# A vision tower on one core: products with Wo in another bank, and three changes of order in attention

## The reference, cut to what matters

```python
h = tokens(x)                                   # 8 x 256 x 512, a state space model's kernel
h = concat([class token, h], axis=1)            # 8 x 257 x 512
h = h + attention(layernorm(h))                 # 16 heads of 32, then out @ Wo.T + bo
h = h + mixture(layernorm(h))                   # 8 experts, the two best of each token

def attention(x):
    q, k, v = x @ Wq.T + bq, x @ Wk.T + bk, x @ Wv.T + bv
    q, k = q * cos(rot), k * sin(rot)
    attn = softmax(q @ k.T / sqrt(32) * spiral)   # by head
    return (attn @ v) @ Wo.T + bo
```

## Time and profile before

| | |
|---|---|
| median of 3 runs | 771.75 us (770.42 to 772.37) |
| the profiled execution | 771.67 us, its span 769.9 us |
| PE busy | 677.3 us, 88% of the span |
| PE weight loads | 544.7 us, 71% |
| DVE busy | 531.5 us, 69% |
| ACT busy | 406.9 us, 53% |
| POOL busy | 148.0 us, 19% |
| mean granted clock of PE | 0.958 |

### The profile page before, as it was taken

The page is one execution under the profiler, slowest core; times in us unless marked ns, Lnnn a source line. Parts: engine busy times, 40 slices in busy tenths (PEclk is TensorE's granted clock), DMA queues, the critical chain, the costliest instruction groups (busy, mean ns, idle before and its releaser), DMA issues.

```text
span 769.9 us, 16642 instructions
## 1 busy us (share of the span) xinstructions
PE 677.3 (88%) x5653; PEld 544.7 (71%) x5654; DVE 531.5 (69%) x1217; ACT 406.9 (53%) x1060; POOL 148.0 (19%) x305
## 2 busy tenths in 40 slices
PE   3758887879999999999999999888479999998898
PEld 3447777867768687777867778655368888886686
DVE  4989795376778678687777777678784444446575
ACT  3835554476767667576766667666513333333111
POOL 5000000110111121111111020021122222227460
PEclk9889999999999999999999999999659999999899
DMA  7400336400001000000100002306716755557794
GB/s 226 160 0 1 139 88 147 112 1 2 3 14 42 0 27 28 27 27 14 41 0 27 27 14 96 111 29 218 274 55 199 207 165 164 164 163 229 240 324 149
DMA packets 54552, 76.11 MB, mean 99 GB/s; under 512 B 24665, under 2 KB 26969, under 8 KB 54386
## 3 DMA queue, kind: packets, MB, share of 16 engines
q1 hardware_dynamic: 41394, 42.56, 17.0%
q0 software_dynamic: 5920, 19.40, 9.8%
q10 hardware_dynamic: 7200, 13.63, 4.7%
HBM read 45.42 MB, written 30.16 MB: 98 GB/s over the span
## 4 chain that ended last, share of the span: by engine, by line
PE 69%; DVE 19%; issue 4%; ACT 3%; DMA 3%; POOL 1%; SPq 0%; DVEq 0%; ACTq 0%; POOLq 0%
PE ps L1939 43%; PE ps L2042 7%; PE ps L2052 4%; PE ps L2035 4%; PE ps L2092 4%; DVE ring L1376 3%; DVE ring L1377 3%; PE ps L1886 2%; DVE negmax L1447 2%; PE ps L2059 1%; DMA b_in<-in_L_tok_B_ri_dram 1%; PE ps L1930 1%; ACT prb L1006 1%; PE ps L2311 1%; DVE ew_lo L1686 1%
## 5 line engine op out<-in xcount | busy, mean ns | idle before, releaser
L1014 ACT ACTIVATE pts<-ps 128x512 f32<-128x512 f32 x128 | 77.2, 603 | 106.4 <-PE ps L2042 106.4
L1006 ACT ACTIVATE prb<-ps,negmax 128x257 f32<-128x257 f32 x256 | 117.9, 479 | 5.1 <-DVE negmax L1447 4.2
L1447 DVE TENSOR_REDUCE negmax<-ps 128x2 f32<-128x514 f32 x128 | 82.5, 686 | 30.7 <-PE ps L2035 30.7
L2042 PE MATMUL ps<-ident,prb 128*128 128x128 f32 x512 | 83.3, 286 | 6.2 <-DVE prb L1456 2.0
L2042 PEld LDWEIGHTS ps<-ident,prb 128*128 128x128 f32 x512 | 56.9, 143 | 30.6 <-issue 11.9
L1456 DVE TENSOR_SCALAR prb<-prb,rrec 128x258 f32<-128x258 f32 x256 | 73.5, 351 | 2.3
L1177 ACT ACTIVATE rows<-ps 128x512 f32<-128x512 f32 x40 | 23.9, 598 | 84.5 <-DVE ps L1798 84.5
L1939 PE MATMUL ps<-ew_hi,xnT_hi 128*128 x160 | 66.8, 418 | 0.1
L1939 PE MATMUL ps<-ew_lo,xnT_hi 128*128 x160 | 63.5, 397 | 0.0
L1939 PE MATMUL ps<-ew_hi,xnT_lo 128*128 x160 | 63.3, 396 | 0.0
L1886 PE MATMUL ps<-ident,ring 128*128 128x128 f32 x384 | 47.7, 281 | 15.7 <-DVE ring L1377 14.1
(11 more groups left out here) (391 smaller groups left out, 1760.9 us busy)
## 6 DMA issues: line engine op xcount, KB each, us to landing
y_slots<-rows ACTq DMA_DIRECT2D x40, 256.0 KB
ew<-in_L_ffn_expert_w_dram SPq DMA_DIRECT2D x8, 1024.0 KB, 8.5
h_dram<-h_ob SPq DMA_DIRECT2D x17, 256.0 KB, 2.0
xn_dram<-tok SPq DMA_DIRECT2D x17, 256.0 KB, 2.2
h_late<-h_dram SPq DMA_DIRECT2D x15, 256.0 KB
out_dram<-h_late SPq DMA_DIRECT2D x14, 256.0 KB
y_slots<-u_sb SPq DMA_DIRECT2D x9, 256.0 KB, 6.9
tok_dram<-so SPq DMA_DIRECT2D x4, 512.0 KB, 3.5
```

What stands on the lines that cost most here:

```text
L1006: e = act.activation(prb[:, u % 2, j, 0:KEYS], ps[:, j, 0:KEYS], ACT.Exp, bias=negmax[:, u % 2, j:j + 1], accum_out=rowsum[:, u % 2, j:j + 1])
L1014: act.activation(pts[:, slot:slot + 2, :, st * P:(st + 1) * P], ps[:, 4, :].rearrange("p (h t s) -> p h t s", h=2, t=HALVES), ACT.Copy).th ...
L1447: dve.tensor_reduce(negmax[:, u % 2, 2 * b:2 * b + 2], ps[:, 2 * b:2 * b + 2, 0:KEYS], AX_X, ALU.max, negate=True).then_inc(s["dve_max"], 1)
L2042: mm = pe.transpose(ps[:, 4, (2 * j + tt) * P:(2 * j + tt + 1) * P], prb[:, u % 2, 2 * b + j, tt * P:(tt + 1) * P], ident[:, :])
```

## The change

- `project` for the first token half of batches 0 to 6 becomes `project_first_half`, into bank 5: the twelve products with Wo first, the class value's product last. It waits for the low parts of `oT` at its start and for `pclsT` before its last product, and no longer for `ptc`. `residual` of that half reads bank 5. `pv(c, 0)` of unit 5, which writes bank 5, waits for this residual.
- `project` for the second half waits for `ptc` and no longer for the first half's residual. `project` in general waits for the low parts only before its last three products.
- In unit 3 the token tile is turned ahead of `key_turn` and `cls_turn`.
- In the last batch DVE takes the low parts (`lo_ot`) ahead of `keep_xnT(6)` in unit 6 and ahead of `take_logits(0)` in unit 7.

```diff
@@ def before_norm(c, u, first, last):
-                if last and u in (4, 5, 6):
+                if last and u in (4, 5):
                     keep_xnT(2 * u - 6)
-                if last and u == 7:
-                    dve.wait_ge(s["loaded_router"], 32)
-                    dve.wait_ge(s["pool_routing_const"], 18)
-                    take_logits(0)
...
                 if u == 4 and not first:
-                    residual(c - 1, 0, 6)
+                    residual(c - 1, 0, 5)
...
                 if u == 6:
                     lo_ot(c, 0)
-                    if not last:
+                    if last:
+                        keep_xnT(6)
+                    else:
                         lo_qk(c + 1, 1)
                 if u == 7:
...
                     lo_ot(c, 1)
-                    if not last:
+                    if last:
+                        dve.wait_ge(s["loaded_router"], 32)
+                        dve.wait_ge(s["pool_routing_const"], 18)
+                        take_logits(0)
+                    else:
                         lo_qk(c + 1, 3)
@@ def project(c, st, bank):
                 pe.matmul(ps[:, bank, :], pclsT[:, w], u_rows[:, :], start=True, stop=False)
                 for ic in range(KC):
+                    if ic == KC - 1:
+                        pe.wait_ge(s["dve_oT_low"], (c + 1) * KC)
                     mm = split3(ps[:, bank, :], (oT_hi[:, ic, w], oT_lo[:, ic, w]),
                                 (woT_hi[:, ic, :], woT_lo[:, ic, :]), False, ic == KC - 1)
                 mm.then_inc(s["pe_projected"], 1)
+
+            def project_first_half(c, bank):
+                pe.wait_ge(s["dve_oT_low"], (c + 1) * KC)
+                for ic in range(KC):
+                    split3(ps[:, bank, :], (oT_hi[:, ic, 0:P], oT_lo[:, ic, 0:P]),
+                           (woT_hi[:, ic, :], woT_lo[:, ic, :]), ic == 0, False)
+                pe.wait_ge(s["dve_key_probs"], 2 * (c + 1))
+                pe.matmul(ps[:, bank, :], pclsT[:, 0:P], u_rows[:, :], start=False, stop=True
+                          ).then_inc(s["pe_projected"], 1)
@@ tensor: def body(c, first, last):
                     if u == 3:
-                        pe.wait_ge(s["dve_cls_step"], 3 * c + 3)
-                        if not first:
-                            key_turn(c - 1)
-                        cls_turn(c)
                         if last:
                             turn_xn(0)
                         else:
                             pe.wait_ge(s["act_v_kept"], c * HALVES + 2)
                             pe.wait_ge(s["dve_xhat"], (c + 1) * HALVES + 1)
                             x_turn(7, 0)
+                        pe.wait_ge(s["dve_cls_step"], 3 * c + 3)
+                        if not first:
+                            key_turn(c - 1)
+                        cls_turn(c)
...
                         if first:
                             pe.wait_ge(s["dve_spread"], 3 + 2 * KC)
+                        else:
+                            pe.wait_ge(s["dve_residual"], c * HALVES - 1)
                         pv(c, 0)
...
                     if u == 3 and not first:
-                        pe.wait_ge(s["dve_key_probs"], 2 * c)
-                        pe.wait_ge(s["dve_oT_low"], c * KC)
+                        project_first_half(c - 1, 5)
+                    if u == 4 and not first:
                         pe.wait_ge(s["dve_cls_pT"], c + 1)
-                        project(c - 1, 0, 6)
-                    if u == 4 and not first:
-                        pe.wait_ge(s["dve_residual"], c * HALVES - 1)
                         project(c - 1, 1, 6)
@@ after the last batch:
             pe.wait_ge(s["dve_key_probs"], 2 * NB)
-            pe.wait_ge(s["dve_oT_low"], NB * KC)
             project(last, 0, 6)
             project(last, 1, 7)
```

## The result

| | before | after |
|---|---|---|
| median | 771.46 us (6 runs, 770.42 to 775.40) | 761.17 us (6 runs, 757.86 to 765.25) |
| ratio | | 0.986, 95% interval 0.9837 to 0.9883 |
| the profiled execution | 771.67 us, span 769.9 | 765.25 us, span 763.5 |
| mean granted clock in it | 0.958 | 0.951 |
| PE busy | 677.3 us | 677.8 us |

What follows compares the result with a forecast made beforehand. PE was taken to bound each middle batch, with only its waits removable: 6 x 1.65 = 9.9 us, plus 0.6 in the last batch, 10.5 from 771.67, giving 761.2 us (own range 759.2 to 762.5; with rivals 1 and 3, 758.5 to 765.0).

Steps and rivals of the forecast that it cites:

- Which waits bound a batch: Units 3 and 4, batches 1 to 6: PE's waits bound a batch; removing 1.35 and 0.30 us saves 1.65 each, 9.9 in all.
- The two edits belong together: Unit 3: token turn starts after v's eviction, and the first half's products follow the turns at 352.84, 1.35 us earlier.
- New waits at nothing: Projections and unit 5's `pv(c, 0)`: the new waits are met beforehand, so they cost 0.
- DVE next, but just not late: Before `top` of units 4 and 5: DVE keeps 0.25 us idle, then runs 0.04 us late, without loss.
- Rival 1: Units 4 and 5: DVE takes over, or PE finds the second wait elsewhere; 8.7 us gained, 763.0 us; chance 0.13.
- Wait for v: Unit 3: the token tile's turn, now first, waits 0.45 us for v's eviction by ACT.
- Rival 4: Unit 3: v's eviction, if later than 353.1, holds the class turns back; slower, 774 us; chance 0.03.
- Rival 2: First half's products don't start early, held by ACT or `pclsT`; only 0.6 us remain, 771 us; chance 0.04.
- Last batch: Batch 7: low part earlier in unit 6 starts `pv(c, 1)` 0.60 us sooner; units 3 and 7 bring 0.
- The 1.57 us before the last projection: End of attention: PE's 1.57 us wait for the last low part goes but brings 0, since DVE is later by 3 us.
- Rival 3: End of attention: idle time grows from 1.77 to about 2.6 us, clock falls, costing 3 us; 764 us; chance 0.12.
- What would have made it wrong: Batches under 1.3 us shorter, a new v or `pclsT` wait over 0.6 us, or clock below 1.00 ending attention.

Runs made afterwards that it cites:

- exchange alone: Kernel before, with only unit 3's order changed (token tile turned ahead of the class rows): 767.01 us, ratio 0.999.
- projection alone: Changed kernel with the order of unit 3 and of the last batch put back: 760.94 us, ratio 0.9903 to the kernel before.
- made large: Changed kernel with ACT's eviction of v's second tile moved behind unit 3's exponentials in batches 1 to 7: 798.91 us in a single execution.
- class value first: Changed kernel with the class value's product put back first in the first half's projection, still in bank 5: 762.24 us, ratio 0.9935 to the kernel before.
- the other two edits alone: Kernel before with only unit 3's token tile turned first: 767.01 us; with only DVE's order in the last batch changed: 766.87 us.
- changed again: The changed kernel, no further edit, run once more on another chip: 757.22 us, ratio 0.9884 to the kernel before.
- split: Changed kernel with products of both projections moved into PE's remaining waits in units 3 and 4: 751.47 us, ratio 0.9797 to the kernel before.

## Why the prediction was right, by its steps

- *Which waits bound a batch.* Right. PE's list of waits in units 3 and 4 gave the gain, and the weight loads gave its size: forecast 1.35 for the start of the projection, measured 1.32; 1.65 for the batch, measured 1.63 to 1.64; 9.9 for six, measured 9.8. The table's 9.69 is between turns of keys, which stand later behind the scores of unit 3 than before, by 0.26 us in batch 7 and by 0.16 in batch 1; between scores of unit 3 it is 9.69 + 0.26 - 0.16 = 9.79.
- *The two edits belong together.* The steps put the exchange behind v's eviction and the products behind the exchange. The runs show what this means: exchange alone 0, projection alone 1.32, both 1.64.
- *The class value's product last has 1.7 us of cover.* Measured 1.6.
- *New waits at nothing.* Right: the wait inside `project`, that before the last product and that before `pv(c, 0)` show no row.
- *DVE next, but just not late.* Right: 0.31 us left where 0.25 was forecast, and none in unit 5. Rival 1 is out: the experiment with products in the gaps took another 0.97 us from the same batch.
- *Wait for v.* 0.52 us of PEld's idle time, forecast 0.45. Rival 4's mechanism exists and was far from its point; made large, it is dearer than I priced it, since the clock adds 2.0 us to each 3.5. Rival 2 was priced too high: the second half's 0.30 us doesn't hang on an early start of the first (unit 4 took 5.52 us with the class value first as well), so 6 x 0.30 + 0.6 = 2.4 us would have remained and not 0.6, 769.3 and not 771.
- *Last batch.* 1.46 became 0.85, forecast 0.86; `turn_xn(1)` took up 0.23 us more (1.31 to 1.54), where I said 0.4, and nothing came of it, as forecast. The stage is 1.08 us shorter, not 0.6. Cut at the scores of the units it comes apart: 0.61 is the low part (scores of unit 6 to scores of unit 7: 5.99 before, 5.38 after), 0.13 lies in unit 4 (6.44 to 6.31), which I had put at zero; the projection alone has it too (6.32), the other two edits alone don't (6.45 each), so it belongs to the second half's projection; and 0.09 is behind the scores of unit 7 (25.66 to 25.57), its cause not looked into; units 3 and 5 are unchanged (8.42 and 8.43, 4.80 and 4.80). The other 0.26 is no time saved, but the place of the cut: `key_turn` stands 2.25 us behind the scores of unit 3 now, 1.99 before, as the tokens' turn is ahead of it. So the last batch gained 0.82 where 0.6 was forecast, and the whole of attention from unit 3 of batch 1 on 9.8 + 0.8 = 10.6, where the sum had 10.5.
- *The 1.57 us before the last projection.* Gone from PE and not in the time: the last turns of tokens still wait, now 2.43 us (forecast 2.6), for DVE.
- *The clock.* Rival 3 is what the profiled execution shows: 2.67 us lost behind attention, forecast 3. Yet it isn't the rule. Idle times of 2.39 to 2.45 us at this place left the stage at 8.57 to 8.59 us in three traces (class value first, changed again, split) and made it 9.78, 10.93 and 11.25 in three others. So the Trainium skill (TensorE: Matmul & The Clock Gate, "HAM oscillation — how this bites in real kernels") agrees in kind, that idle gaps bring the clock down, and a gap of this length decides nothing by itself. In the four traces with a shorter idle time there (0.27 to 1.80 us) the clock never fell, so the longer gap may have made a fall more likely; ten traces don't settle it. With 6 runs of either kernel the median falls on 761.17, where the forecast had 761.2. That they agree within 0.1 is luck, given a spread of 7 us of the runs, and in the sum two small misses offset each other (0.1 too much in the batches, 0.2 too little in the last one).
- *What would have made it wrong.* The first two signs (batches under 1.3 us shorter, a new wait over 0.6 us) didn't appear. The third, a clock below 1.00 behind attention, did in the profiled execution, and cost 2.67 us against a price of 3; the gain of the batches stood beside it.

## What to carry to other kernels

Lay out the bound engine's waits as a chain before valuing an edit: a wait removed alone may only lengthen the next one (0.0 us here), and be worth 0.3 us once that one is gone. An accumulation can take its late operand last (1.21 us of a batch here). By the code that needed a bank other than the one that the late operand is made from. Where a total scatters by several microseconds, a period between the same two operations in the trace measures an edit much more finely: here two traces of one kernel gave 44.31 us both, as long as the clock stayed at 1.00 in the batches.

## What the runs showed of the hardware that was not expected

- Making PE's wait in each batch 3.5 us longer (3.8 in place of 0.3) cost 5.5 us a batch: the clock fell to its low level in or just behind each of these waits (mean 0.94 to 0.95 from one `key_turn` to the next), and the four turns behind one took 1.11 us in place of 0.60.
- The same idle time (2.4 us) at the same place was followed by 1.2 GHz in three of six traces and by 2.4 GHz in the other three. Shorter ones were too, now and then: one of 1.56 us before the last projection in one trace of three, one of 1.21 us in unit 7 of the last batch in one of seven.
- Six products moved among the turns shortened the batch by 0.97 us: more than the 0.7 us that the matmuls' rows show as waits, less than the 1.42 that the weight loads show. Here the waits of the matmul rows understate what PE gained; what a change between products and turns costs isn't shown.
